# Transformer kernel on one core: attention weights applied in two halves of the queries, an earlier start of the transposed scores, and other issuers for two kinds of transfer

## The reference

```python
qkv = (zn @ W_qkv + b_qkv).reshape(b, n, 3, H, DH)          # H = 16, DH = 16, n = 1024
scores = jnp.einsum('bhqd,bhkd->bhqk', q, k) * scale
attn = jax.nn.softmax(scores, axis=-1)
msa = jnp.einsum('bhqk,bhkd->bhqd', attn, v)
out = msa_cat @ W_proj + b_proj
return z + out                                              # then layer norm, FFN, layer norm
```

## Time and profile before

| | |
|---|---|
| median of 3 runs | 1864.62 us (1864.11 to 1867.95) |
| the profiled execution's own time | 1860.18 us |
| its span, first to last instruction | 1858.5 us |
| mean granted TensorE clock | 0.912 of 2.4 GHz |
| busy: TensorE matmuls (PE) / DVE / ACT | 1614.6 / 1275.2 / 825.5 us |

### The profile page before, as it was taken

The page is one execution under the profiler, slowest core; times in us unless marked ns, Lnnn a source line. Parts: engine busy times, 40 slices in busy tenths (PEclk is TensorE's granted clock), DMA queues, the critical chain, the costliest instruction groups (busy, mean ns, idle before and its releaser), DMA issues.

```text
span 1858.5 us, 25769 instructions
## 1 busy us (share of the span) xinstructions
PE 1614.6 (87%) x7834; PEld 924.4 (50%) x7834; DVE 1275.2 (69%) x2551; ACT 825.5 (44%) x1255; POOL 307.6 (17%) x367
## 2 busy tenths in 40 slices
PE   5969999993899996979999788899986988999786
PEld 2758888883443324644333356433334744333354
DVE  3672322212689977958998687788968958997586
ACT  1302233230357773342776624266772333776522
POOL 0243222213000222000004030100323000000020
PEclk8989999997779998996999989789998987999898
DMA  3227867763312200022222000412200031210000
GB/s 127 68 68 226 263 227 226 233 213 119 65 22 36 64 24 1 1 46 48 36 36 70 1 1 2 92 19 36 64 25 1 1 63 32 40 30 1 1 1 23
DMA packets 86203, 123.08 MB, mean 66 GB/s; under 512 B 16474, under 2 KB 62811, under 8 KB 86059
## 3 DMA queue, kind: packets, MB, share of 16 engines
q1 hardware_dynamic: 74058, 97.92, 20.2%
q0 software_dynamic: 12000, 23.35, 4.4%
HBM read 76.84 MB, written 18.61 MB: 51 GB/s over the span
## 4 chain that ended last, share of the span: by engine, by line
PE 65%; DVE 19%; issue 6%; ACT 3%; DMA 3%; POOL 2%; SPq 1%; DVEq 0%; ACTq 0%; POOLq 0%
PE PS L925 12%; PE PS L968 11%; DVE MX L1418 10%; PE PS L845 7%; PE PS L857 7%; PE PS L1050 6%; PE PS L1060 5%; PE PS L955 2%; PE PS L911 2%; PE PS L796 2%; DMA Qs<-MR 2%; ACT Pb L676 1%; PE PS L1011 1%; PE PS L1080 1%; PE PS L902 1%
## 5 line engine op out<-in xcount | busy, mean ns | idle before, releaser
L1418 DVE TENSOR_REDUCE MX<-PS 128x1 f32<-128x512 f32 x1024 | 636.3, 681 | 86.9 <-PE PS L925 86.1
L676 ACT ACTIVATE Pb<-PS 128x1024 f32<-128x1024 f32 x512 | 498.4, 1023 | 200.5 <-PE PS L955 199.8
L925 PE MATMUL PS<-Ks,Qs 48*128 48x512 f32 x1024 | 389.6, 496 | 43.3 <-DVE MX L1418 12.4
L925 PEld LDWEIGHTS PS<-Ks,Qs 48*128 48x128 f32 x1024 | 177.4, 203 | 362.0 <-DVE MX L1418 324.1
L955 PE MATMUL PS<-Qs,Ks 50*128 50x512 f32 x1024 | 308.8, 450 | 12.3 <-DMA Qs<-MR 7.5
L968 PE MATMUL PS<-Pb,V 128*32 128x512 f32 x2048 | 281.7, 623 | 2.7 <-ACT Pb L676 2.7
L955 PEld LDWEIGHTS PS<-Qs,Ks 50*128 50x128 f32 x1024 | 144.8, 192 | 64.2 <-ACT Pb L676 51.5
L497 POOL DMA_DIRECT2D Qs<-MR x128 | 66.0, 523 | 652.3 <-DVE MR L1431 375.7
L1318 DVE TENSOR_TENSOR V<-PS,V 128x512 f32<-128x512 f32 x39 | 26.9, 691 | 203.1 <-PE PS L857 203.1
L857 PE MATMUL PS<-Pb,OT 128*128 128x256 f32 x624 | 141.0, 379 | 0.0
L603 ACT ACTIVATE OT<-PS,b1t 128x256 f32<-128x256 f32 x156 | 65.5, 471 | 158.7 <-PE PS L845 158.7
(11 more groups left out here) (278 smaller groups left out, 1861.7 us busy)
## 6 DMA issues: line engine op xcount, KB each, us to landing
Pb<-W SPq DMA_DIRECT2D x78, 512.0 KB, 3.8
y_slot<-V SPq DMA_DIRECT2D x39, 256.0 KB, 3.8
Qs<-Qh SPq DMA_DIRECT2D x128, 64.0 KB, 2.3
Ks<-Kh SPq DMA_DIRECT2D x128, 64.0 KB, 2.3
V<-b SPq DMA_DIRECT2D x39, 128.0 KB, 3.6
XT<-x_mid POOLq DMA_DIRECT2D x4, 1024.0 KB, 6.3
out<-X SPq DMA_DIRECT2D x4, 1024.0 KB, 4.6
OT<-xT SPq DMA_DIRECT2D x2, 1024.0 KB, 6.3
```

The lines of the kernel that those rows point to most:

```text
L676: F["ex"].inc(act.activation(Pb[:, kt % 2, 2 * qh:2 * qh + 2, :], PS[:, 2 * qh:2 * qh + 2, :], ACT.Exp, scale=0.25))
L925: F["slp"].inc(pe.matmul(PS[:, slot_bank(i), :], Qs[rows, p % NB, t * P:(t + 1) * P], Ks[rows, p % NB, kh * HALF:(kh + 1) * HALF], start=T ...
L1418: F["sld"].inc(dve.tensor_reduce(MX[:, p % 2, a, t, kh:kh + 1], PS[:, slot_bank(i), :], AX.X, ALU.max))
```

## The change

1. **Weighing in halves.** `weigh(m)` becomes `weigh(m, qh)`: each call makes 4 products of 256 columns for one half of the queries and waits only for that half's exponential. The order of the queries inside `Qh` is changed so that the result lands in the same places of bank 7. ACT's waits (`pv`) follow the halves, and its `evac_o` moves between the two exponentials of a pair's first step. TensorE's loop becomes: one unit of maxima, transposed scores, one unit, half of the weighing, twice in a step; and the two heads of the transposed scores are issued in the order (1, 0).
2. **The early lead.** The first five `values(t)` are made before any unit of maxima (`EARLY = 5`, in other banks), the remaining three after 8, 16 and 24 units. The turn of the first pair's maxima comes after 1 more unit (`SOON`) where it was 4, and the main loop begins 6 units ahead (`START`) where it was 12; it then issues 5 units a step until it is 12 ahead again. ACT takes the first two units of Q of the next sequence before and between its last late rows.
3. **Issuers.** The rows of maxima are transferred by SP, 2 transfers for a pair, between its stacks; the output is stored by POOL, which also waits for its landing; SP goes on to the next stacks without that wait. POOL's gathers for the next sequence are issued in one go.

Other lines of the diff (`C["..."].wait(eng, n)` written as `eng.wait_ge(C["..."].sem, n)`) give the same instructions.

```diff
@@ transposed scores, weighing and main loop, TensorE
-                    for a in range(2):
+                    for a in (1, 0):
...
-                def weigh(m):
+                def weigh(m, qh):
...
-                    F["ex"].wait(pe, b, 2 * m + 2)
-                    for qh in range(2):
+                    F["ex"].wait(pe, b, 2 * m + qh + 1)
+                    for c in range(2):
                         for a in range(2):
-                            j = 2 * a + qh
-                            ins = pe.matmul(PS[32 * j:32 * j + 32, 7, :], V[:, kt, 2 * p + a, :], Pb[:, kt % 2, 2 * qh + a, :],
-                                            start=(kt == 0), stop=(kt == KT - 1), skip_group_check=True)
+                            j = 2 * a + c
+                            ins = pe.matmul(PS[32 * j:32 * j + 32, 7, qh * QW:(qh + 1) * QW], V[:, kt, 2 * p + a, :],
+                                            Pb[:, kt % 2, 2 * qh + a, c * QW:(c + 1) * QW],
+                                            start=(kt == 0 and qh == 0), stop=(kt == KT - 1), skip_group_check=True)
...
-                values(0)
-                maxima(3)
+                for t in range(EARLY):
+                    values(t)
+                F["vv"].wait(pe, b, EARLY - 1)
                 F["qkv"].wait(pe, b, 8)
-                for t in range(1, TT):
-                    maxima(6 * t - 2)
+                for t in range(EARLY, TT):
+                    maxima(8 * (t - EARLY + 1))
                     values(t)
...
-                maxima(UN + LEAD)
+                maxima(UN + START)
...
-                    ahead = UN + LEAD + 4 * m
-                    transposed_scores(p, kt, 0)
-                    maxima(ahead + 2)
-                    transposed_scores(p, kt, 1)
-                    maxima(ahead + 3)
-                    if m:
-                        weigh(m - 1)
-                    maxima(ahead + 4)
+                    ahead = UN + min(LEAD + 4 * m, START + 5 * m)
+                    step = UN + min(LEAD + 4 * (m + 1), START + 5 * (m + 1)) - ahead
+                    for qh in range(2):
+                        maxima(ahead + 2 * qh + 1)
+                        transposed_scores(p, kt, qh)
+                        maxima(ahead + (step if qh else 2))
+                        if m:
+                            weigh(m - 1, qh)
@@ SP: the row of maxima
+                def maxima_row(p):
+                    F["sld"].wait(sp, b, turn_slot(p) + 1)
+                    if p >= NB:
+                        F["bp"].wait(sp, b, 2 * KT * (p - NB + 1))
+                    hold(sp, "sp")
+                    for a in range(2):
+                        r, at = ROW * a + STACK, 2 * a * TT
+                        F["mrow"].inc(sp.dma_start(
+                            Qs[r:r + 2, p % NB, :].rearrange("o (t q) -> o t q", t=TT).bitcast(F32),
+                            MR[at:at + 2 * TT, p % 2, :].bitcast(F32)), by=16)
+
+                for p in range(NB):
+                    stack(p)
+                maxima_row(0)
+                for p in range(NB, NP):
+                    maxima_row(p - NB + 1)
+                    stack(p)
+                for p in range(NP - NB + 1, NP):
+                    maxima_row(p)
@@ ACT
-                                F["pv"].wait(act, b, (n - 4) // 2 + 1)
+                                F["pv"].wait(act, b, n - 3)
...
-                        if kt == 0 and p > 0:
-                            evac_o(p - 1)
+                            if kt == 0 and p > 0 and qh == 0:
+                                evac_o(p - 1)
...
+                late_root(1)
+                if more:
+                    F["xw"].wait(act, b, TT, 1)
+                    qk_evac(b, 1, (0,))
+                late_rows(1, (4, 5))
+                if more:
+                    qk_evac(b, 1, (1,))
+                late_rows(1, (6, 7))
@@ POOL, end of a sequence (before: by SP)
+                F["xa"].wait(pool, b, TT - 2 + TT // 2)
+                F["xd"].wait(pool, b, 2 + TT // 2)
+                hold(pool, "pool")
+                F["outd"].inc(pool.dma_start(out.rearrange("(n p) d -> p n d", p=P)[:, bass.ds(b * TT, TT), :], X[:, :, :]), by=16)
+                F["outd"].wait(pool, b, 16)
```

More of the change, by code:

```diff
@@ L20 @@
 HALF = 512
+QW = HALF // 2
 NH = S // HALF
@@ L411, in _, with stack @@
             with sp.Fori(0, B) as b:
-                for p in range(NP):
+                def stack(p):
                     k = p % NB
@@ L637, in turned, with qk_evac, late_root @@
                                                scale=lnw[:, c:c + 1], bias=lnb[:, c:c + 1]))
+            def qk_evac(b, ahead, units):
+                for u in units:
+                    F["qkp"].wait(act, b, u + 1, ahead)
+                    c, w, th = u // 4, (u % 4) // 2, u % 2
+                    dst = (Kh if w else Qh)[:, c, th * HALF:(th + 1) * HALF]
+                    F["qka"].inc(act.activation(dst, PS[:, u % 4, :], ACT.Identity,
+                                                bias=bqkv[:, w * DC + c:w * DC + c + 1]))
             def sequence(b, more):
                 def evac_o(p):
-                    F["pv"].wait(act, b, KT * (p + 1))
+                    F["pv"].wait(act, b, 2 * KT * (p + 1))
                     F["ov"].inc(act.activation(OP[:, p, :], PS[:, 7, :], ACT.Copy))
-                def late_norm(i):
+                def late_root(i):
                     F["vel"].wait(act, b, i + 1)
@@ L736, in _ @@
             turned(0, 0)
+            F["xw"].wait(act, 0, TT)
+            qk_evac(0, 0, (0, 1))
             with act.Fori(0, B - 1) as b:
@@ L767, in _ @@
             ins.then_inc(s_proT, 1)
-            C["hm"].wait(pe, 1)
+            pe.wait_ge(C["hm"].sem, 1)
             for o in range(DC):
@@ L782, in _ @@
             C["hw"].inc(ins)
-            C["hw"].wait(pe, 2)
+            pe.wait_ge(C["hw"].sem, 2)
             pe.wait_ge(s_scan, 2)
@@ L816, in _ @@
                     ranks(0)
-                    C["rd"].wait(pe, 1)
+                    pe.wait_ge(C["rd"].sem, 1)
                 state_out(h)
@@ L831, in x_turn @@
                 if k:
-                    C["te"].wait(pe, k)
+                    pe.wait_ge(C["te"].sem, k)
                 for c in range(DC):
@@ L906, in values @@
                 def values(t):
-                    if t >= 2:
-                        F["vv"].wait(pe, b, t - 1)
+                    same = [k for k in range(t) if value_bank(k) == value_bank(t)]
+                    if same:
+                        F["vv"].wait(pe, b, same[-1] + 1)
+                    if t == EARLY:
+                        F["qkv"].wait(pe, b, 8)
                     for kc in range(DC):
-                        ins = pe.matmul(PS[:, 7 - 4 * (t % 2), 0:D], XT[:, kc, t * P:(t + 1) * P], wqkv[:, kc, 2 * D:3 * D],
+                        ins = pe.matmul(PS[:, value_bank(t), 0:D], XT[:, kc, t * P:(t + 1) * P], wqkv[:, kc, 2 * D:3 * D],
                                         start=(kc == 0), stop=(kc == DC - 1))
@@ L1102, in _ @@
             pro(dve.memset(Hz[:, :, :], 0.0))
-            C["hm"].wait(dve, 1)
+            dve.wait_ge(C["hm"].sem, 1)
             for b in range(B):
@@ L1106, in _ @@
             pro(ins)
-            C["wgs"].wait(dve, 1)
+            dve.wait_ge(C["wgs"].sem, 1)
             for c in range(DC):
```

194 lines of the change are left out of this document (88 added, 106 removed).

## The result

The changed kernel takes 1914.68 us (median of 4 runs, 1913.13 to 1938.71); the kernel before, on the same chip, 1866.28 us (4 runs, 1864.11 to 1876.47). The ratio is 1.0289 [1.0245, 1.0333]: slower by 2.9%. The profiled execution took 1913.31 us at a mean granted clock of 0.863 (before 0.912). The forecast was 1803 us.

The account below looks back on a forecast made before the run. Neither engine was full: the loop of bank, unit, weighing, unit set the step. Terms -59.4 - 7 + 3 + 1.7 = -61.7 us gave 1798.5 us profiled, 1803 us median with 4.4 added; range 1783 to 1838 us.

Parts of the forecast that it names:

- tails: After each sequence's last maxima: halved weighing no longer delays the next scores, 1.8 us a sequence, -7 us, bounds 0 and 12.
- four first pairs: First pair of each sequence: 23.4 us instead of 26.8 through the earlier main loop, bounds 21 and 29.
- twenty-four other pairs: Six pairs after the first in each sequence: 20.9 us a pair instead of 22.6, 125.4 for six.
- start of the first sequence: First units go out behind four `values` instead of one, 3.4 us later: +3 us, once.
- last store: End of the kernel: POOL's store lands after 6.3 us, SP's after 4.6; only the last is on the path, +1.7 us.
- Halves remove that: 10 steps x 0.14: Tail: ACT's 0.27 us idle per four exponentials goes; with 0.4 from a shorter last block, 1.8 us a sequence.
- two such steps: First pair: two five-unit steps at the lower clock, each losing 1.5 us, 3.0 us in its 23.4.
- The rival for it: First pair: lower clock for all six five-unit steps, +24 us, 1827; chance 0.18 together with late rows.
- The one of a halved block that keeps its length: Weighing: halves bound by issue, not columns; 1897 us at 0.85 us a half, 1966 at 1.00; chance 0.07.
- The rule on weight loads: Weighing: second four loads exposed in each half, half 0.67 us, step 2.64, kernel 1833 us; chance 0.16.
- The early start: Before the first pair: first transposed scores 4.8 us after the negated maxima instead of 10.8, main loop about 6 us earlier.
- The issuers at nothing: Transfers by SP and POOL: queue free in time, store hidden except the last; no gain counted at sequence starts.

## Why the prediction was wrong

The sum was made for a profiled execution: 1798.5 us; measured 1913.31, 114.8 more. By its own terms (the start is counted from the first turn of the sequence's rows to its first maximum):

| term | forecast | measured |
|---|---|---|
| tails | -7 | 170.1 - 104.6 = +65.5 |
| four first pairs | 93.6 in all | 111.2 |
| twenty-four other pairs | 501.6 | 524.2 |
| start of the first sequence | +3 | 28.2 - 23.9 = +4.3 |
| last store | +1.7 | 126.7 - 124.5 = +2.2 |

The misses are 72.5, 17.6, 22.6, 1.3 and 0.5 us, together 114.5; the other stages make up the rest.

- **The step that failed is "Halves remove that: 10 steps x 0.14"**, the tail, bounded between 0 and 12 us of gain. The term kept, without saying so, the clock of the tail before (0.94), as if it belonged to the stage. It depends on what TensorE does there, and the edit changed just that. The trace before had the warning in it: the clock falls at the last turn there too, and only its return kept the loss small. The run with the two halves side by side, the same instructions, brings 42.6 back to 29.8 us, and whole blocks to 28.4: this is shown, not argued. What the chip goes by when it gives the clock back is not shown, and neither is whether scores and halves in turn would keep a full clock that had not fallen at the turn.
- **The clock of the first pair** was seen as a risk, with "two such steps" at 1.2 GHz. It was the whole pair and a part of the next. The rival for it was priced at +24 us; it cost 17.6, and some 14 of the 22.6 (the second pair takes 27.9 us in the first sequence and 23.8 in the others, instead of 21.2). Of the 17.6, the order of the halves makes 9.8 (the first pairs take 101.4 us in all with halves side by side); the other 7.8 stand there as well, so two slow steps were too few by themselves. The condition named at the end of the prediction, that the clock stays down through the first pair, came true; that it could stay down in the tail was no rival at all.
- **No rival had the result's place.** The one of a halved block that keeps its length gave 1897 to 1966 us, and 1914.68 lies in there, but by accident: at full clock a half is 0.57 us, and at 1.2 GHz 1.01, as the block's scaling said.
- **The mechanism of the halves was right**, with its sizes: half 0.57 (forecast 0.57), half step 1.24 (1.21), step 2.48 (2.42), pair 21.24 at full clock (20.9); the last makes 24 x 0.34 = 8.2 us of the miss. DVE still waits 11.7 us a sequence where under 6 was named. The rule on weight loads, quoted there from the Trainium skill ("TensorE: Matmul & The Clock Gate", "The mechanism"), would have made it 0.67: this kernel's row does not show that second load.
- **The early start and the last store** came about nearly as summed: the first transposed scores of the second sequence start 4.3 us behind the negated maxima (4.8 forecast), the starts of the later sequences are unchanged (22.3 to 22.4 us, before 22.1 to 22.7), and the last store costs 2.2 us. **The issuers at nothing** was a miss in the other direction: alone they gain some 12 us in the medians, 0.9932.

The Trainium skill ("TensorE: Matmul & The Clock Gate", "HAM oscillation — how this bites in real kernels") puts a clock that is lost again and again down to gaps in which TensorE idles, waiting for a DMA. The trace agrees in part: the clock falls behind a gap, though one of 1.86 us in which TensorE waits for DVE. That it stays down doesn't fit: 39.00 of 39.00 us are busy at 0.50, while the neighbour in the other order idles more at 0.83. Here the measurement decides.

## What to carry to other kernels

Before halving a block of products, ask of each stage it runs in at which clock it stands, where the clock falls and returns, and what else fills TensorE there: in the middle, among maxima, the halves gave 0.992, and in the tails they lost 65.5 us. Edit by stage, and read the granted clock of each stage after. And where TensorE comes out of a wait at the low clock, try the order that keeps short blocks together: here it gave back 53.0 us of the tails with the same instructions.

## What was not expected of the hardware

- A stretch with products in flight without a pause (39.00 us) stayed at 1.2 GHz. Scores of 50 rows and eight instructions of the weighing took turns in it; with sixteen in a row the clock came back (1.00 from 1039.4 on), and so it did with one more product of 512 columns each time (0.90).
- A stretch kept at full clock by 12 unread products lost it at the turn of the maxima right behind them (0.66 over 1.5 us, then 0.50); this way of warming up ahead of the loop bought nothing.
- With halves side by side or whole blocks, the same instructions in the first pair took 23.5, 25.0 or 27.9 us in different sequences of one execution, at a clock of 0.70 to 0.50. Why one and not the other stays open.
